# Attention with a masked softmax on one core: ScalarE's share of the block moves goes from behind the exponentials to a place in front of them

## The reference

```
def _gat_layer(x, W, adj):
    proj = x @ W                              # W: 256 x 512
    Wh, Ws = jnp.split(proj, 2, axis=-1)
    scores = Wh @ Ws.T                        # 4096 x 4096
    a = jax.nn.softmax(scores, axis=-1) * adj
    out = a @ Wh
    out = out + x
    return jax.nn.leaky_relu(out, NEG_SLOPE)

y = _gat_layer(_gat_layer(x, W[0], adj), W[1], adj)
out = _layernorm(x + y, axis=-1)
```

## Time and profile before

| what | value |
|---|---|
| median of 3 runs | 1680.99 us (1677.59 to 1681.62) |
| profiled execution: time, span | 1675.62 us, 1673.7 us |
| busy PE, DVE, POOL, ACT | 1588.3, 1233.2, 917.6, 678.8 us |
| mean granted TensorE clock | 0.99 of full speed |
| DMA | 302.59 MB, mean 181 GB/s |

### The profile page before, as it was taken

One profiled execution on the slowest core, in us unless ns is written; L12 is line 12 of the kernel. 1 busy time (PEld: TensorE's weight loads), 2 busy tenths in 40 slices (PEclk: granted clock), 3 DMA queues, 4 the chain that ended last, 5 costly groups with the idle time before them and its releaser, 6 DMA issues.

```text
span 1673.7 us, 23474 instructions
## 1 busy us (share of the span) xinstructions
PE 1588.3 (95%) x8104; PEld 1319.3 (79%) x8104; DVE 1233.2 (74%) x1558; ACT 678.8 (41%) x1175; POOL 917.6 (55%) x935
## 2 busy tenths in 40 slices
PE   7899999999999999999788999999999999999996
PEld 6778888888788888887677888888788888877885
DVE  4567777777777777777636788778878888787785
ACT  4333444444434444444333444344434444434442
POOL 2355555555555555555444555555555555555565
PEclk9999999999999999999999999999999999999998
DMA  5357767777767776768913777777677777777774
GB/s 182 86 147 185 193 185 184 186 198 182 184 186 192 184 186 187 195 186 220 261 32 105 193 192 184 192 201 194 177 191 202 196 186 189 197 190 185 199 192 126
DMA packets 167750, 302.59 MB, mean 181 GB/s; under 512 B 39760, under 2 KB 68432, under 8 KB 167504
## 3 DMA queue, kind: packets, MB, share of 16 engines
q1 hardware_dynamic: 105808, 132.75, 32.3%
q0 software_dynamic: 36864, 134.23, 27.6%
q10 hardware_dynamic: 24960, 34.11, 8.4%
HBM read 157.29 MB, written 9.44 MB: 100 GB/s over the span
## 4 chain that ended last, share of the span: by engine, by line
PE 55%; DVE 22%; ACTq 7%; POOL 6%; ACT 5%; issue 3%; DMA 1%; SPq 0%; POOLq 0%
PE banks L443 18%; PE banks L336 9%; PE banks L338 9%; PE banks L337 9%; PE banks L445 9%; DVE neg_max L641 8%; DVE ring L669 7%; ACTq L242 7%; POOL a_lo L766 6%; DVE ring L674 4%; ACT a_hi L559 3%; ACT ring L540 1%; DMA turned<-ring 1%; DVE weight L660 1%; DVE wh L605 1%
## 5 line engine op out<-in xcount | busy, mean ns | idle before, releaser
L766 POOL TENSOR_TENSOR a_lo<-turned,a_hi 128x512 fp32r<-128x512 f32 x512 | 718.4, 1419 | 667.3 <-ACT a_hi L559 666.8
L443 PE MATMUL banks<-wh,a_hi 128*128 128x512 f32 x2048 | 753.6, 406 | 50.7 <-POOL a_lo L766 43.2
L540 ACT ACTIVATE ring<-banks,neg_max 128x1024 f32<-128x1024 f32 x256 | 286.0, 1117 | 815.2 <-DVE neg_max L641 815.2
L445 PE MATMUL banks<-wh,a_lo 128*128 128x256 f32 x2048 | 577.5, 282 | 0.0
L443 PEld LDWEIGHTS banks<-wh,a_hi 128*128 128x128 f32 x2048 | 387.9, 189 | 182.6 <-POOL a_lo L766 83.0
L641 DVE TENSOR_REDUCE neg_max<-banks 128x1 f32<-128x1024 f32 x256 | 310.9, 1214 | 261.8 <-PE banks L338 261.8
L336 PE MATMUL banks<-x_t,q_t 128*128 128x512 f32 x1024 | 405.8, 396 | 4.0 <-DVE x_t L605 2.4
L338 PE MATMUL banks<-x_t,q_t 128*128 128x512 f32 x1024 | 401.8, 392 | 0.0
L337 PE MATMUL banks<-x_t,q_t 128*128 128x512 f32 x1024 | 400.9, 391 | 0.0
L445 PEld LDWEIGHTS banks<-wh,a_lo 128*128 128x128 f32 x2048 | 390.0, 190 | 5.8
L669 DVE SCALAR_TENSOR_TENSOR ring<-ring,weight,load 128x1024 f32<-128x1024 f32 x256 | 377.0, 1472 | 7.3 <-DMA load<-adj 4.6
(11 more groups left out here) (68 smaller groups left out, 729.6 us busy)
## 6 DMA issues: line engine op xcount, KB each, us to landing
load<-adj POOLq DMA_DIRECT2D x256, 512.0 KB, 5.0
turned<-ring SPq DMA_DIRECT2D x1528, 64.0 KB, 4.0
turned<-ring ACTq DMA_DIRECT2D x520, 64.0 KB, 4.0
ring<-x SPq DMA_DIRECT2D x8, 512.0 KB, 5.0
rows<-x SPq DMA_DIRECT2D x32, 128.0 KB, 4.3
x_scratch<-rows SPq DMA_DIRECT2D x32, 128.0 KB, 3.9
rows<-x_scratch SPq DMA_DIRECT2D x32, 128.0 KB, 4.3
first_rows<-x SPq DMA_DIRECT2D x32, 128.0 KB, 4.0
```

The lines of the kernel that those rows point to most:

```text
L443: nc.tensor.matmul(psum[:, bank, :], a_hi[:, s, b], wh[:, k].rearrange("p a d -> p (a d)"), start=start, stop=stop, skip_group_check=True)
L445: last = nc.tensor.matmul(psum[:, bank, 0:D], a_lo[:, s, b], wh[:, k, 0], start=False, stop=stop, skip_group_check=True)
L540: nc.scalar.activation(ring[:, i % RING, :].rearrange("p (b e) -> p b e", b=2), psum[:, 2 * (i % 2):2 * (i % 2) + 2, :], ACT.Exp, bias=neg ...
L766: nc.gpsimd.tensor_tensor(a_lo[:, j % 2].rearrange("p b (r j) -> p b r j", r=QUADS), as_f32(turned[:, unit % 2, :, b:b + SUB, :]).rearrang ...
```

## The change

ACT's two moves of a chunk, which stood behind the exponentials of the same step, now stand behind the step's two splits and in front of its exponentials. The computation of the four chunk factors, which stood right behind the exponentials of step 4t+3, becomes a function of its own that is called at the start of step 4t, in front of that step's splits; between its old and its new place there were the moves of step 4t+3, which are gone from there, and the copies of side products of that step, which occur in steps 3 and 7 of the first layer and step 3 of the second alone. The drained chunks, the other engines' programs, the shares of the moves and all waits of a move or an exponential stay as they are.

```
--- before.py
+++ after.py
@@ exponentials(i), on ScalarE
                 nc.scalar.activation(ring[...], psum[...], ACT.Exp, ...).then_inc(exp_done, 1)
-                if c == CPT - 1:
-                    all_of = slice(t % 2 * CPT, (t % 2 + 1) * CPT)
-                    act.wait_ge(row_max_done, t + 1)
-                    nc.scalar.activation(factor[:, all_of], neg_max[:, all_of], ACT.Exp,
-                                         bias=row_neg_max[:, t % 2:t % 2 + 1], scale=-1.0).then_inc(factor_done, 1)
+
+            def chunk_factors(t):
+                all_of = slice(t % 2 * CPT, (t % 2 + 1) * CPT)
+                act.wait_ge(row_max_done, t + 1)
+                nc.scalar.activation(factor[:, all_of], neg_max[:, all_of], ACT.Exp,
+                                     bias=row_neg_max[:, t % 2:t % 2 + 1], scale=-1.0).then_inc(factor_done, 1)
@@ the loop over steps, on ScalarE
             for step in range(STEPS):
-                k = chunk_at(step - LAG_PRODUCT)
+                k, summed = chunk_at(step - LAG_PRODUCT), tile_at(step - CPT)
+                if summed is not None:
+                    chunk_factors(summed)
                 if k is not None:
                     split_a(2 * k)
                     split_a(2 * k + 1)
+                for m in weighed_at(step):
+                    if not is_drained(m):
+                        move_blocks(m)
                 for m in weighed_at(step - 1):
                     if is_drained(m):
                         move_blocks(m)
...
                 i = chunk_at(step)
                 if i is not None:
                     exponentials(i)
-                for m in weighed_at(step):
-                    if not is_drained(m):
-                        move_blocks(m)
                 for side in sides_after(step):
                     split_side(side)
```

## The result

The changed kernel takes 1748.04 us (median of 4 runs, 1745.07 to 1750.67) against 1679.98 us before: a ratio of 1.0402, 95% interval 1.0383 to 1.0420. It is 68 us slower where 17 us faster was forecast. The span of the profiled execution grew from 1673.7 to 1746.5 us.

What follows compares the result with a forecast made beforehand. TensorE, 95% busy, was taken as the bound, with 0.82 us of stops per tile; 0.16 + 0.14 saved in 47 tiles (14.1 us) plus 2.5 us in 13 others gave 1681.0 - 16.6 = 1664.4 us, range 1655 to 1679.

Steps and rivals of the forecast that it cites:

- The step that failed: Step 4t: split follows the factors, 1.30 not 1.46 behind the exponentials; a_lo, weighing, turn and maximum 0.16 us earlier.
- the signs that the prediction named for being right: Step 4t: split at 1.30, weighing 2.1 to 2.3, moves 1.2, next split 1.11 behind exponentials; a_lo wait about 65 us.
- The trade at the shared inputs: Step 4t: DVE's weighing and POOL's a_lo exclude each other; rival with weighing first everywhere: no change, 1676 us, chance 0.13.
- The second gain: Moves of step 4t before their exponentials: turn's end to split of step 4t+1 2.43 instead of 2.57, 0.14 us gained.
- the stated upper bound of 1.41: Step 4t: a pair of moves as slow as 1.41 instead of 1.17 gives 2.67, a loss of 0.10 us.
- The third rival: Step 4t: SP's moves, ACT's moves and POOL's load start together, ACT's pair takes 2.31: slower, 1720 us, chance 0.12.
- that wait in step 4t+2: Moves before exponentials wait for POOL's second a_lo; exponentials 0.60 late in a bad case, 1.3 us remain, priced at nothing.
- Steps 4t+1 and 4t+2: Moves in front of these steps' exponentials: covered by time ACT stands anyway or by TensorE's later need, priced at nothing.

Runs made afterwards that it cites:

- The spare copy: Changed kernel plus one ScalarE copy of 128x4 elements that nobody reads, between the factors and the splits of step 4t: 1685.28 us, ratio 1.0042.
- the single columns: Changed kernel with DVE's 128x4 weight instruction written as four of 128x1: 1680.11 us, ratio 1.0011.
- the first experiment: Kernel before, with only the moves of steps 4t+3 put in front of their exponentials: 1736.99 us, ratio 1.0359.

## Why the prediction was wrong

**The step that failed** is the sentence "The `a_lo` starts 0.16 earlier and stays ahead of the weighing", with the bounds "0.05 to 0.16" behind it. The 0.16 came, to the hundredth. But the sentence looked only at the weighing (ready at 2.28 behind the exponentials) as what meets the `a_lo` at 2.02. The timeline of VectorE had a weight instruction at 305.88, which is 2.01 behind 303.87. That row was not among those the prediction rested on: a 0.23 us instruction, priced at nothing. With it in view the prediction's own figures give no answer: the `a_lo` at 1.30 plus 0.72, 2.02, against the weight instruction at 2.01 is a tie. The `a_lo` came first, by 0.01 to 0.03 in the 61 tiles where the instruction was held. In place of 0.16 gained, the turn came 1.07 later (319.63 is 6.90 behind the exponentials, 309.70 was 5.83). The run of steps 4t+3 alone shows its size, 59 us; the spare copy and the single columns each take it away in another way.

The trace of the kernel before already held one such case, in a step 4t whose `a_lo` (1465.50) started ahead of the weight instruction:

```profile
1465.52 1.29 DVE L660 TENSOR_SCALAR weight<-factor,row_inv 128x4 f32<-128x4 f32 x1
```

This one row is why the group above has a mean of 247 ns and not 230. And several of the signs that the prediction named for being right were met while the kernel got slower: the split at 1.30, weighings of 2.1 to 2.3, the split 1.11 behind the exponentials. None of its signs, right or wrong, looked at the instruction in front of the weighing.

**The trade at the shared inputs** was itself described rightly, and even named as a rival, but with the order turned only one way (the `a_lo` later). The earlier side was given no rival, since earlier seemed safe.

**The second gain** was mis-sized. Its sum was 0.03 + 1.17 + 0.12 + 1.11 = 2.43. Measured in the tile above: the moves start 0.03 behind the turn (right), the pair takes 1.42, the queue 0.12 (right: 321.08 to 321.20), the split comes 1.10 behind (right); 2.67. The pair was the one wrong term, and the stated upper bound of 1.41 was its real value: a loss of 0.10, as the bound said. The third rival, three queues at one moment, comes nearest to it, at a fifth of its price (0.25 more for the pair, not 1.14). But only two queues start together in the changed kernel: POOL's load is let go by the weighing and starts at 318.64, 0.99 before the turn ends.

**The moves of step 4t** hid another term: in the tiles in which POOL comes second, ACT then waits for POOL. I had priced that wait in step 4t+2 alone. It shows in the run of these moves alone (16 tiles) and plays next to no part in the changed kernel, where the `a_lo` comes first in nearly every tile, as predicted.

**Steps 4t+1 and 4t+2** were right at nothing, together 0.9995 (0.9982 to 1.0007).

**Parts and whole.** 59 us (steps 4t+3), 8 us (steps 4t) and nothing that can be told from noise (the others, 2 us faster by the medians) make 65 to 67; the change cost 68. The factors' new place was never tested alone; in the first experiment they stay in their old place and the loss is nearly the same.

## What to carry to other kernels

Where two engines share inputs that one instruction holds to its end, an instruction that starts earlier is not a gain until every instruction of the other engine in that window has been listed, the small ones first: here one of 0.23 us, met 0.01 us too late, cost 1.1 us in nearly every tile. If a step lies that near to a flip (0.16 moved, 0.17 in hand), give the case beyond the flip a rival with its own price. A transfer's issue that stands between two instructions on the path is best put behind the second one, where it runs beneath that engine's work, rather than in front of the first: here 20 us faster against 8 us slower.

## What the runs showed of the hardware that was not expected

A pair of transfers issued by ScalarE takes longer when it starts at the same moment as the sync engine's: 1.40 to 1.42 us against mostly 1.16 to 1.18 inside SP's stream. ScalarE and then the sync engine in the changed kernel, steps 4t to 4t+2:

```profile
319.66 1.42 ACTq L242 DMA_DIRECT2D turned<-ring  x2
...
323.24 1.16 ACTq L242 DMA_DIRECT2D turned<-ring  x2
...
329.53 1.40 ACTq L242 DMA_DIRECT2D turned<-ring  x2
```

```profile
319.65 7.59 SPq L242 DMA_DIRECT2D turned<-ring  x12
327.28 0.58 SPq L266 DMA_DIRECT2D x_scratch<-rows  x1
329.52 8.60 SPq L242 DMA_DIRECT2D turned<-ring  x12
```

The slow pairs start 0.01 behind SP's first issue, and the fast one starts inside its row of twelve. Over the whole trace, 168 pairs start within 0.05 us of an SP issue in front of which SP stood idle, with a median of 1.41, and 84 start inside its stream, with a median of 1.16. The place in ScalarE's program isn't the reason: the kernel before has 15 such common starts, with a median of 1.39. Why a common start is worse than an overlap stays open; no run separates the two queues.
